# A decoder layer on one core: from unit 13 of 16 the engines' written orders put attention first, and the first half's exponents go behind the last unit

## The chip, the core and the metric

The kernel runs on one core of a Trainium2 chip. The core has five engines with a queue each: TensorE (PE, matmuls), VectorE (DVE), ScalarE (ACT), GpSimd (POOL) and SyncE (SP, which issues the transfers here). Each engine works through its own list in the order in which the program writes it, and waits for semaphores that other engines raise. The metric is the device time of one execution in microseconds (us), lower is better.

## What is computed

One decoder layer on x of 8 batches x 128 tokens x 128 features, in float32:

```python
x = x + attention(layernorm(x))          # 16 heads of 8, causal, score = -beta * distance(q, k)
x = x + mlstm(layernorm(x), ctx, ctx)    # 4 heads of 32, queries from x, keys and values from ctx
x = x + experts(layernorm(x))            # router over 8 experts, top 2, each silu(g) * u, then down
```

The score of the attention is a function of the squared distance between query and key. With `ed = sqrt(|q|^2 - 2qk + |k|^2 + eps)`, it is one of three formulas, chosen by `ed < 0.1` and `ed > 2`, and a softmax over the keys follows. The second block's weights are built from gates:

```python
log_D = cumsum(log_sigmoid(f))[t] - cumsum(log_sigmoid(f))[s] + i[s]       # for s <= t
C = (q @ k.T) / sqrt(32) * exp(log_D - max_s(log_D))
h = C / (max(|sum(C)|, exp(-max_s(log_D))) + 1e-6) @ v                     # then a norm over each head
```

The gates `i` and `f` are 8 columns of a product of [x, ctx, ctx] with a 384 x 8 matrix.

## The kernel before

**Three stages.** The attention is worked in 16 *units* (numbers 0 to 15; two units of 8 heads for each batch). Then the second block and the router are worked in two *halves* of four batches (half 0 is batches 0 to 3, half 1 is batches 4 to 7). Then 16 expert products follow: `z` 0 to 7 are the eight experts for half 0, `z` 8 to 15 those for half 1.

**The attention pipeline.** Every engine runs `step(s)` for s up to 20, and in a step each engine works on several units at different stages. The distances of unit s+1 and s+2 are made on PE (`scores`). ACT takes squares, logarithms and exponentials of them. DVE makes the chosen formula of unit s (L1011, L1018, L1036), and then the *far selection* of unit s-1 (L1071), which writes `dist`. POOL adds the causal mask to unit s-1 (L596, L599) and makes the comparison for a later one (L607). DVE takes the row minima of unit s-2 (L1030, then two small subtractions L1046, L1063). PE turns the minima (below called `minima`, into PM), ACT copies them into `shift` (L801), PE transposes `dist` and adds the shift in ten matmuls (`weights`, into P3), ACT makes the exponential (L773, `pT`), PE multiplies with the values (`values`, into PO). At the end of each batch follow on DVE a copy, a reciprocal and a product (L1004, L1021, L1040), on PE a transpose, on ACT a copy (`oT`, L778), on PE the product with `wo`, and on DVE the sum L1053 that writes a batch of the first residual, `x1`. Its statistics are `stat(b)` (L1078, L1079). All matmuls stand under L1352, the helper `mm`.

**The second block.** For half c its stages are `front(c, 0..7)`: the rstd (ACT), normed rows `xn` (L913 to L916, L951 on DVE), their transpose `xT` (PE, then L817 on ACT), the gate products from the context (`of_context`, 8 matmuls) and from the rows (8 matmuls), their sum on DVE (L1092 to L1099), three functions on ACT (L821 to L823), a difference (L1102), the cumulated sum on PE, `aT` (L1105, L1106), its transpose, a running maximum (L1112) and `rblk` (L1116, L1119). Each is one hop from engine to engine with little work in it. Then for each batch m of the half: `ex(m)` on PE (the exponents, two matmuls of 512 columns), `rows(m)` on ACT (four exponentials of 128 columns, L834), `qk(m)` on PE (128x512 in float32), `rows(m)` on DVE (the product L1130), `outs(m)` on PE (into 33 columns for each head) and `outs(m)` on ACT (L844, L845). There is one PSUM bank for `qk`, so `qk(m+1)` waits for the L1130 of batch m. When all four batches of half 0 are out, the DVE stages `head(0, 0, 0..6)` follow: denominator (L1158 to L1161), variance (L1167 to L1169), gain (L1176), root, product (L1197), the sum into `x2` (L1205), statistics (L1212, L1215). Then `back(0, 5)` makes normed rows again (L913 to L951), PE transposes them, ACT copies them and rounds them to `xhi`, DVE makes `xlo` (L1271), and the router follows.

**Where the order comes from.** The tables `ACT_AT`, `DVE_AT` and `PE_AT` say for a step and a place in it which of these stages the engine runs there; a call of `at(s, place)` does it. `(21, 1)` is the last place before the experts, `(22 + z, ...)` lies inside them. In before, half 0's `front` stages lie at steps 13 to 16, its `ex`, `qk`, `rows` and `outs` at steps 15 to 20, and `head` between the stages of `front(1, ...)` at `(20, 5)` on DVE. PE has the whole chunk 1 (`ex`, `qk`, `outs` 4 to 6) ahead of the first expert product.

**Filler matmuls.** `stay_warm(n)` on PE issues n matmuls of 512 columns that nobody reads. `WARM` gives their number ahead of `ex(4)` and of the stages 1 to 5 of `front(1, ...)`: 7, 5, 2, 6, 1, 0.

**POOL** runs its attention steps up to s = 16, copies half 0's `xT` into a block layout at s = 14 (`blocks(0)`), makes `centre(0)` at s = 16, then waits for the expert weights (`exp_in`) and splits them for z = 0, 1 (`prepare`: a cast and a subtraction of 128x512), then `blocks(1)`, `centre(1)`, and the other splits beside the experts.

## Time and profile before

| | us |
|---|---|
| median of 3 runs | 255.01 (254.7 to 256.24) |
| the profiled execution | 257.45, of which the span on the core is 255.6 |
| busy: PE, DVE, ACT, POOL | 198.8 (78%), 190.6 (75%), 157.1 (61%), 112.0 (44%) |

The chain that ended last spends 52% of the span on PE, 21% on DVE, 12% on ACT and 13% in gaps in which nothing visible was waited for. The profile page's rows of tenths give 40 slices of 6.4 us. DVE is at 9 or near it up to slice 16 (about 105 us), PE from slice 26 on (about 166 us); between these two stretches no engine is full. A time in a row is counted from the span's start; "idle before" is how long the engine stood before the row, with what ended it.

### The profile page before, as it was taken

How to read it: one execution, taken by the hardware profiler on the slowest of the kernel's cores; microseconds unless marked ns; L12 is line 12 of the kernel's file. 1: busy time of each engine (PE TensorE's matmuls, PEld its weight loads, DVE VectorE, ACT ScalarE, POOL GpSimd, SP SyncE). 2: the span in 40 equal slices, each digit the busy share in tenths (PEclk: the TensorE clock that was granted, in tenths of full speed). 3: DMA queues.
4: the chain of work that ended last, by engine and by line, in shares of the span. 5: the costliest groups of instructions: out<-in, count | busy, mean ns of one | idle time of the engine just before them, and what ended most of it. 6: DMA issues, size and time to landing. Idle time of an engine off the chain costs nothing.

```text
span 255.6 us, 6401 instructions
## 1 busy us (share of the span) xinstructions
PE 198.8 (78%) x2340; PEld 151.8 (59%) x2341; DVE 190.6 (75%) x532; ACT 157.1 (61%) x319; POOL 112.0 (44%) x151
## 2 busy tenths in 40 slices
PE   0697442744758669768798896999999898999995
PEld 0263132534546457557555752478988797888884
DVE  6868899995799999997757389673786943656554
ACT  2499989992999999785256221565555549332320
POOL 9730365673446654447126018002367744734000
PEclk9999955555897775665579868899999999999999
DMA  4305674884068149400000400000000000100001
GB/s 116 94 1 133 155 188 128 223 210 107 9 220 255 32 109 348 132 3 0 3 1 3 167 1 0 0 3 0 0 3 1 1 3 0 41 1 3 0 3 42
DMA packets 28396, 17.49 MB, mean 68 GB/s; under 512 B 11588, under 2 KB 26444, under 8 KB 28108
## 3 DMA queue, kind: packets, MB, share of 16 engines
...
## 4 chain that ended last, share of the span: by engine, by line
PE 52%; DVE 21%; issue 13%; ACT 12%; DMA 1%; DVEq 0%; ACTq 0%
PE P L1352 36%; PE PO L1352 12%; PE PM L1352 4%; DVE dist_mem L1018 3%; DVE xn L951 2%; DVE dist L1071 2%; DVE nm L1030 1%; ACT dist_mem L795 1%; DMA x_sb<-x 1%; ACT split_mem L718 1%; DVE dist_mem L1036 1%; DVE wgu L977 1%; ACT sqn L784 1%; DVE split_mem L1130 1%; DVE dist_mem L1011 1%
## 5 line engine op out<-in xcount | busy, mean ns | idle before, releaser
L1313 DVE SCALAR_TENSOR_TENSOR dist_mem<-P,gub,dist_mem 128x512 f32<-128x512 f32 x32 | 23.8, 749 | 24.8 <-ACT dist_mem L873 24.5
L873 ACT ACTIVATE dist_mem<-P,gub 128x512 f32<-128x512 f32 x32 | 21.9, 689 | 30.9 <-PE P L1352 30.9
L607 POOL TENSOR_SCALAR m_gt<-dist_mem 128x640 uint8<-128x640 f32 x16 | 29.0, 1814 | 6.0 <-issue 4.0
L1352 PEld LDWEIGHTS PO<-proj_mem,dist_mem 128*128 128x128 f32 x244 | 29.4, 192 | 1.2 <-DVE ctx_sb L1331 0.2
L1352 PE MATMUL PO<-proj_mem,dist_mem 128*128 128x128 f32 x244 | 30.0, 276 | 0.0
L1352 PE MATMUL P<-cf,dist 128*128 128x128 f32 x80 | 22.9, 369 | 6.5 <-ACT shift L801 6.5
L596 POOL TENSOR_TENSOR dist<-dist,cf 128x128 f32<-128x128 f32 x16 | 7.3, 457 | 46.6 <-DVE dist L1071 46.6
L1352 PE MATMUL P<-xhi,whi 128*128 128x512 f32 x64 | 26.5, 415 | 1.1 <-DVE dist_mem L1313 1.1
L1352 PE MATMUL P<-xhi,wlo 128*128 128x512 f32 x64 | 25.1, 392 | 0.0
L1352 PE MATMUL P<-xlo,whi 128*128 128x512 f32 x64 | 25.0, 391 | 0.0
L1352 PEld LDWEIGHTS P<-cf,dist 128*128 128x128 f32 x80 | 14.9, 186 | 12.1 <-ACT shift L801 9.5
L657 POOL TENSOR_TENSOR wlo<-wgu,whi 128x512 fp32r<-128x512 f32 x16 | 20.4, 1274 | 3.2 <-POOL whi L654 3.2
L1352 PE MATMUL P<-shift,cb 128*128 128x128 bf16 x80 | 20.6, 274 | 0.0
L654 POOL CAST whi<-wgu 128x512 fp32r<-128x512 f32 x16 | 10.3, 646 | 21.6 <-PE P L1352 21.6
L1352 PE MATMUL P<-stn,stq 128*32 128x256 bf16 (+3 forms) x256 | 10.9, 315 | 11.0 <-DVE dist_mem L1018 10.8
L1352 PE MATMUL P<-stk,stq 128*32 128x256 bf16 (+3 forms) x256 | 10.8, 311 | 10.0 <-issue 6.9
L665 POOL TENSOR_TENSOR ctx_sb<-ctx_sb,dist_mem 128x512 f32<-128x512 f32 x8 | 10.4, 1301 | 17.8 <-ACT dist_mem L881 17.8
L1352 PEld LDWEIGHTS P<-stn,stq 128*32 128x32 bf16 x256 | 7.3, 122 | 15.4 <-issue 14.8
L1030 DVE TENSOR_REDUCE nm<-dist 128x2 f32<-128x256 f32 (+1 forms) x64 | 15.5, 305 | 0.8 <-POOL dist L599 0.7
L1352 PE MATMUL PO<-vab,proj_mem 128*32 128x9 f32 (+1 forms) x896 | 13.8, 193 | 2.0 <-ACT proj_mem L773 1.9
L1352 PEld LDWEIGHTS PO<-vab,proj_mem 128*32 128x32 f32 x896 | 12.5, 132 | 3.7 <-ACT proj_mem L773 2.2
L1352 PEld LDWEIGHTS P<-stk,stq 128*32 128x32 bf16 x256 | 7.8, 129 | 11.3 <-issue 10.8
...
## 6 DMA issues: line engine op xcount, KB each, us to landing
...
```

The lines of the kernel that those rows point to most:

```text
L596: pool.tensor_tensor(ends, ends, cm.unsqueeze(1).unsqueeze(1).broadcast_to([128, 2, 2, ST]), ALU.add)
L607: pool.tensor_scalar(m_gt[:, g.k % 2, :], e2[:, g.k % 2, :], 4.0 - ATT_EPS, None, ALU.is_gt).then_inc(sm["gt_done"], 1)
L654: pool.tensor_copy(hi, w).then_inc(sm["whi_done"], 1)
L657: pool.tensor_tensor(lo, w, hi, ALU.subtract).then_inc(sm["w_ready"], 1)
L665: pool.tensor_tensor(chunk(acc, 0), chunk(acc, 0), yw[:, :, :], ALU.add).then_inc(sm["added"], 1)
L873: A(sil[:, f, :], (P1, P2)[f][:, 0, :], ACT.Silu, bias=gub[:, 0, one:one + 1]).then_inc(sm["sil_done"], 1)
L951: V.tensor_scalar(xn[:, b, :], src[:, c * CB + b, :], mv[:, p, b, 0:1], rs[:, p, 4, b:b + 1], ALU.subtract, ALU.mult).then_inc(sm["xn_done ...
L1018: V.copy_predicated(wt[:, p, :], m_ge[:, p, :], P2f).then_inc(sm["sel_done"], 1)
L1030: last = V.tensor_reduce(m[:, strip, :], strip_of(d, strip), AX.X, ALU.min, negate=True)
L1071: V.copy_predicated(dist[:, far.k % 4, :], m_gt[:, far.k % 2, :], da[:, far.k % 2, :]).then_inc(sm["dist_done"], 1)
L1313: V.scalar_tensor_tensor(hT[:, z % 2 * 2 + f, :], (P1, P2)[f][:, 1, :], gub[:, 1, one:one + 1], sil[:, f, :], ALU.add, ALU.mult).then_inc( ...
L1352: return nc.tensor.matmul(out_, lhsT, rhs, start=start, stop=stop, **more)
```

## The change

It writes the lists of all four compute engines anew from unit 13 on.

- **Half 0's gate stages** are spread over steps 13 to 19, one hop for each place: the context products in two pairs at step 14, the row products in two pairs at steps 14 and 15, the cumulated sum, transposes and maximum at steps 16 to 18.
- **Half 0's exponents** (`ex`, `qk`, `rows`, `outs` 0 to 3) move from steps 15 to 20 behind the last unit, to `(20, 2)` on PE and ACT and `(20, 5)` on DVE, between the stages of `front(1, ...)`; only `ex(0)` stays at step 18.
- **`head(0, ...)`** stood between `front(1, ...)` stages on DVE, and now stands behind `front(1, 6)`, all seven parts together.
- **The far selection of unit 15** is at the start of step 16 on DVE instead of near its end; on PE `minima(15)` is moved to the end of step 16 and `weights(15)` ahead of `values(14)`.
- **Fillers:** WARM is 6, 0, 0, 0, 0, 0, and the six write to PO after the last `x1`.
- **POOL:** `prepare(0)` runs at s = 13, `blocks(0)` and `centre(0)` at s = 16; the subtraction of the first two splits is cut in four parts of 128 columns.

```diff
-WARM = (7, 5, 2, 6, 1, 0)
+WARM = (6, 0, 0, 0, 0, 0)
...
-          (13, 7): [("front", 0, 1)], (14, 7): [("front", 0, 3)],
-          (15, 3): [("front", 0, 4), ("front", 0, 5), ("front", 0, 6)], (16, 1): [("stat", 4)],
+          (13, 7): [("front", 0, 1)], (16, 7): [("front", 0, 3)],
+          (17, 6): [("front", 0, 4), ("stat", 4), ("stat", 5)], (17, 7): [("front", 0, 5), ("front", 0, 6)],
...
+                parts = 4 if z <= POOL_BLOCKS else 1
...
+            for s in range(-1, NU + 1):
+                step(At(None, s))
+                if s in (0, 2):
+                    spread(s // 2)
+                if s == 13:
+                    pool.wait_ge(sm["exp_in"], 48)
+                    prepare(0)
+                if s == NU:
+                    blocks(0)
+                    centre(0)
...
             def step(s):
                 k_ = s.k
                 low, far, near = s - 2, s - 1, s + 1
                 t = s - 4
+                if far.k == NU - 1:
+                    far_selection(far)
...
-                if far.there():
-                    wait(dve, "ds_done", far.n(1))
-                    wait(dve, "gt_done", far.n(1))
-                    wait(dve, "da_done", far.n(1))
-                    pass_waits(dve)
-                    V.copy_predicated(dist[:, far.k % 4, :], m_gt[:, far.k % 2, :], da[:, far.k % 2, :]).then_inc(sm["dist_done"], 1)
+                if far.there() and far.k < NU - 1:
+                    far_selection(far)
...
+                if k_ == NU + 1:
+                    weights(s, s - 2)
+                values(s, s - 3)
+                at(k_, 3)
+                if k_ <= NU:
+                    minima(s, s - 2)
+                at(k_, 4)
+                if k_ <= NU:
+                    weights(s, s - 2)
+                if k_ == NU:
+                    minima(s + 1, s - 1)
...
             def stay_warm(n):
 
+                if n:
+                    pe.wait_ge(sm["x1_done"], B)
                 for _ in range(n):
-                    mm(P2[:, 0, :], ident_b, cb[:, 0:512])
+                    mm(PO[:, :], ident_b, cb[:, 0:512])
```

DVE before, in step 15 from the minima of unit 13 on; `gf`, `aT`, `runmax` and `rblk` are half 0's gates, L1036 and L1040 are attention:

```order
L1030 TENSOR_REDUCE nm<-dist 128x2 [waits nmT_full,causal_done]
L1030 TENSOR_REDUCE nm<-dist 128x2 x3
L1102 TENSOR_TENSOR gf<-gf 128x16 [waits l1p_done]
L1105 COPY gf<-P 128x16 [waits cs_full]
L1106 TENSOR_TENSOR aT<-gpre,P 128x16
L1112 SCALAR_TENSOR_TENSOR runmax<-P,cf 16x128 [waits ar_full]
L1116 TENSOR_TENSOR runmax<-runmax 16x128 [waits rm_done]
L1116 TENSOR_TENSOR runmax<-runmax 16x128 [waits chain_d]
L1119 TENSOR_TENSOR rblk<-runmax,cb 80x512 [waits chain_d]
L1036 SCALAR_TENSOR_TENSOR dist_mem<-dist_mem 128x640 [waits lp_done,sel_done]
L1040 TENSOR_TENSOR o_n<-o_sb,o_rec 128x128 [waits o_rec_done]
```

DVE after, the same place (L1040 is the minima, L1046 the product, L999 the far selection, L1063 the batch of `x1`):

```order
L1040 TENSOR_REDUCE nm<-dist 128x2 [waits nmT_full,causal_done]
L1040 TENSOR_REDUCE nm<-dist 128x2 x3
L1046 SCALAR_TENSOR_TENSOR dist_mem<-dist_mem 128x640 [waits lp_done,sel_done]
L1050 TENSOR_TENSOR o_n<-o_sb,o_rec 128x128 [waits o_rec_done]
L1056 TENSOR_TENSOR nm<-nm 128x8 [waits nm0_done]
L1063 TENSOR_TENSOR x_sb<-PM,x_sb 128x128 [waits wo_full]
L1073 TENSOR_TENSOR nm<-nm 128x8 [waits nm1_done]
L999 COPY_PREDICATED dist<-m_gt,dist_mem 128x640 [waits da_done,ds_done,gt_done] x2
```

Seven gate instructions have left the place between the minima and the product, and the far selections of units 14 and 15 stand one behind the other.

DVE before, from the last batch's statistics on (L1158 to L1169 are the head norm of half 0, L913 to L951 half 1's normed rows):

```order
L1078 BN_STATS bst<-x_sb 128x6 [waits x1_done]
L1079 BN_AGGR mv<-bst 128x2 [waits chain_d]
L1158 SCALAR_TENSOR_TENSOR hden<-split_mem,enm 128x16 [waits enm_done,hs_done]
L1159 TENSOR_TENSOR hden<-hden,split_mem 128x16 [waits chain_d]
L1160 TENSOR_SCALAR hden<-hden 128x16 [waits chain_d]
L1161 RECIPROCAL hden<-hden 128x16 [waits chain_d]
L913 TENSOR_TENSOR rs<-rs 128x4 [waits r0_done,chain_d]
L914 SCALAR_TENSOR_TENSOR rs<-mv,rs 128x4 [waits chain_d]
L915 TENSOR_SCALAR rs<-rs 128x4 [waits chain_d]
L916 TENSOR_TENSOR rs<-rs 128x4 [waits chain_d]
L951 TENSOR_SCALAR xn<-x_sb,mv,rs 128x128 [waits tr_full,chain_d]
L951 TENSOR_SCALAR xn<-x_sb,mv,rs 128x128 x3
```

DVE after, behind the same statistics (L1136 is a batch's product of half 0, L914 to L952 the normed rows of half 1, L1098 and L1099 the gate sums):

```order
L1136 SCALAR_TENSOR_TENSOR split_mem<-P,split_mem 128x512 [waits dT_done,qk2_full]
L914 TENSOR_TENSOR rs<-rs 128x4 [waits r0_done]
L915 SCALAR_TENSOR_TENSOR rs<-mv,rs 128x4 [waits chain_d]
L916 TENSOR_SCALAR rs<-rs 128x4 [waits chain_d]
L917 TENSOR_TENSOR rs<-rs 128x4 [waits chain_d]
L952 TENSOR_SCALAR xn<-x_sb,mv,rs 128x128 [waits tr_full,chain_d]
L952 TENSOR_SCALAR xn<-x_sb,mv,rs 128x128 x3
L1136 SCALAR_TENSOR_TENSOR split_mem<-P,split_mem 128x512 [waits dT_done,qk2_full]
L1098 TENSOR_TENSOR gpre<-P,gb 128x32 [waits gc_full]
L1099 COPY vmean<-P 128x16 [waits chain_d]
L1136 SCALAR_TENSOR_TENSOR split_mem<-P,split_mem 128x512 [waits hh_full,dT_done,qk2_full]
L1103 TENSOR_TENSOR gpre<-gpre,P 128x32 [waits g_full]
```

The head norm has gone from here to behind `rblk`, and the four batch products of half 0 have come in its place.

PE before, from the last product with `wo` on; `wg` is the context product of half 1, `cb` alone are fillers, `xn` the transposes of the normed rows:

```order
L1352 MATMUL PO<-wo_sb,oT 128x128 [waits oT_done]
L1352 MATMUL P<-wg,split_mem 128x12 [waits ctx_in,pT_done]
L1352 MATMUL P<-wg,split_mem 128x12 x3
L1352 MATMUL P<-cb 128x512 x5
L1352 MATMUL P<-cf,xn 128x128 [waits xn_done]
L1352 MATMUL P<-cf,xn 128x128 x3
L1352 MATMUL P<-cb 128x512 x2
L1352 MATMUL P<-wg_raw,xT 128x8 [waits pT_done,vmean_done,xT_done,ctx_in]
L1352 MATMUL P<-wg_raw,xT 128x8 x3
L1352 MATMUL P<-cb 128x512 x6
L1352 MATMUL P<-gf,tri 128x16 [waits lf_done]
L1352 MATMUL P<-cb 128x512
```

PE after, from the same product on (`split_mem` is `qk`, `cb` with `rblk` is `ex`, `ctx` is `outs`):

```order
L1358 MATMUL PO<-wo_sb,oT 128x128 [waits oT_done]
L1358 MATMUL P<-split_mem 128x512 [waits sel_done,blk_done]
L1358 MATMUL P<-cb 128x512 [waits em_done]
L1358 MATMUL P<-rblk,cb 128x512
L1358 MATMUL P<-split_mem 128x512 [waits cT_done]
L1358 MATMUL P<-ctx,split_mem 128x33 [waits cT_done,centred]
L1358 MATMUL P<-ctx,split_mem 128x33 x3
L1358 MATMUL P<-wg,split_mem 128x12 [waits pT_done,ctx_in]
L1358 MATMUL P<-wg,split_mem 128x12 x3
L1358 MATMUL P<-cf,xn 128x128 [waits xn_done]
L1358 MATMUL P<-cf,xn 128x128 x3
L1358 MATMUL P<-cb 128x512 [waits dT_done]
```

The fillers are gone, and half 0's exponents stand ahead of half 1's context product and between its later stages.

## Rows read from the trace of the kernel before

**Rows 1.** Busy time of each engine in three stretches: start:end, length, each engine.

```profile
103.50:147.30 43.80, 36.31 (x537) 26.66 (x537) 31.80 (x93) 23.50 (x62) 17.66 (x27) 0.69 0.10 37
147.30:162.40 15.10, 12.11 (x45) 5.77 (x47) 13.76 (x54) 3.29 (x13) 6.30 (x7) 0.75 0.00 1
162.40:171.40 9.00, 8.73 (x51) 5.83 (x49) 5.49 (x28) 6.16 (x22) 0.00 (x0) 1.00 0.01 2
```

**Rows 2.** Timeline of DVE, steps 13 to 15: start, us, engine, line.

```profile
109.44 1.61 DVE L951 TENSOR_SCALAR xn<-x_sb,mv,rs 128x128 f32<-128x128 f32 x4
...
117.26 0.19 DVE L1092 TENSOR_TENSOR gpre<-P,gb 128x32 f32<-128x32 f32 x1 [1.23 <-PE P L1352]
...
118.46 0.81 DVE L1011 SCALAR_TENSOR_TENSOR dist_mem<-dist_mem,P 128x640 f32<-128x640 f32 x1
...
124.24 0.81 DVE L1036 SCALAR_TENSOR_TENSOR dist_mem<-dist_mem 128x640 f32<-128x640 f32 x1
```

**Rows 3.** Timeline of DVE: far selection of unit 15, last batch of x1.

```profile
131.79 0.89 DVE L1071 COPY_PREDICATED dist<-m_gt,dist_mem 128x640 f32<-128x640 uint8 x1
...
147.03 0.29 DVE L1053 TENSOR_TENSOR x_sb<-PO,x_sb 128x128 f32<-128x128 f32 x1 [1.74 <-PE PO L1352]
```

**Rows 4.** Timeline of PE: qk twice, outs, transposes twice, the first expert product.

```profile
128.51 1.91 PE L1352 MATMUL P<-split_mem 128*128 128x512 f32 x2
...
133.81 1.12 PE L1352 MATMUL P<-split_mem 128*128 128x512 f32 x2 [0.19 <-DVE split_mem L1130]
...
144.25 1.31 PE L1352 MATMUL P<-ctx,split_mem 128*128 128x33 f32 x8
...
150.69 1.06 PE L1352 MATMUL P<-cf,xn 128*128 128x128 f32 x4
...
162.84 0.60 PE L1352 MATMUL P<-cf,xn 128*128 128x128 f32 x4
...
171.37 0.48 PE L1352 MATMUL P<-xhi,whi 128*128 128x512 f32 x1
```

**Rows 5.** Timeline of DVE, second phase: head norm, rblk, last normed rows.

```profile
147.78 0.16 DVE L1158 SCALAR_TENSOR_TENSOR hden<-split_mem,enm 128x16 f32<-128x16 f32 x1
147.98 0.18 DVE L1159 TENSOR_TENSOR hden<-hden,split_mem 128x16 f32<-128x16 f32 x1
...
155.29 0.69 DVE L1197 TENSOR_TENSOR split_mem<-split_mem 128x512 f32<-128x512 f32 x1
...
157.72 0.86 DVE L1212 BATCH_NORM_STATS2 bst<-x_sb 128x6 f32<-128x128 f32 x4
158.62 0.38 DVE L1215 BATCH_NORM_AGGREGATE mv<-bst 128x2 f32<-128x6 f32 x4
...
159.96 0.69 DVE L1119 TENSOR_TENSOR rblk<-runmax,cb 80x512 bf16<-80x512 bf16 x1
...
161.35 1.11 DVE L951 TENSOR_SCALAR xn<-x_sb,mv,rs 128x128 f32<-128x128 f32 x4
```

**Rows 6.** Timeline of ACT: rows(0), and the rstd ahead of back(0, 5).

```profile
131.86 1.09 ACT L834 ACTIVATE split_mem<-P,aT 128x128 f32<-128x128 f32 x4
...
159.10 0.30 ACT L693 ACTIVATE rs<-mv,eps_col 128x4 f32<-128x4 f32 x1 [3.40 <-DVE mv L1215]
159.43 0.21 ACT L694 ACTIVATE rs<-rs 128x4 f32<-128x4 f32 x1
```

**Rows 7.** PE in five stretches: start:end, length, busy, granted clock, DMA.

```profile
112.00:130.00 18.00, 14.92 (x180) 0.50 0.01 1
131.00:144.00 13.00, 11.56 (x228) 1.00 0.20 82
145.00:151.00 6.00, 5.35 (x20) 0.50 0.01 1
155.00:157.00 2.00, 0.03 (x1) 1.00 0.00 0
158.60:161.60 3.00, 3.00 (x8) 0.50 0.00 0
```

137 lines of the change are left out of this document (66 added, 71 removed).

## The prediction

> **What bounds the kernel now.** I read the busy times by stretch first. From step 13 to the last batch of `x1` (103.5 to 147.3 us) no engine is full: PE 36.3, DVE 31.8 and ACT 23.5 of 43.8 us; this is the *tail*, where engines hand small pieces to each other. From there to the end of the normed rows of `back(0, 5)` (147.3 to 162.4, the *second phase*) DVE is busy for 13.76 of 15.10 us. From 162.4 to the first expert product PE is busy for 8.73 of 9.00 us [rows 1]. From the first product at 171.37 [rows 4] to the end of the span, 255.6, PE is the bound (84.2 us), and its list is the same afterwards. So the change is worth what it does to the start of that product. I call the end of the last `x1` T (147.03 + 0.29, about 147.3 [rows 3]) and the end of `back(0, 5)` E (161.35 + 1.11, about 162.4 [rows 5]). The sum has three terms: the move of T, the growth of T to E, the growth of E to the product.
>
> **Term 1, the tail.** Before, DVE starts step 15 at 118.46, having waited 1.23 us for the gate products of PE and run four small gate instructions from 117.26 on. In step 15 seven gate instructions and their hops stand ahead of L1036, which starts at 124.24 [rows 2]; the far selection of unit 15 comes at 131.79, and T 15.5 us later [rows 3].
>
> After the change I walk it forward with the same durations. Step 13 ends later, since the rstd of the normed rows now stands behind ACT's place 5: about 0.7 us, so L951 ends at 109.44 + 1.61 + 0.7 = 111.8 [rows 2]. Step 14 is then 5.1 us of DVE work without a wait (before, from the end of L951 at 111.05 to the instruction ahead of the wait, 117.26 - 1.23 = 116.0: 5.0 us [rows 2]), and so is most of step 15; there DVE waits about 0.8 us for the `wo` product. Step 15 ends at about 122.7. The exponential that the far selection of unit 15 needs stands behind ACT's `shift` of unit 13 and ends at about 123.7. So this selection starts at 123.7, 8.1 us earlier. Behind it stand the minima of 14, the sum L1053 of unit 11 (it waits for PE until 127.3), half 0's gate sums (0.65) and the minima of 15, which end at 129.2. PE takes them only behind `weights(14)`, at 130.6; then come two gate hops (cumulated sum and transpose, to 132.2), `weights(15)` (1.8 at half clock), the exponential (0.8), `values(15)` with the copy ahead of it (to 136.3), a transpose, `ex(0)`, two `wo` products with their copies, each with a hop: T at 140.3. That is 16.6 us behind the selection, where before had 15.5. PE's items in this walk are at half clock, 1.2 GHz, because the granted clock was 0.50 from 112 to 130, though PE was busy for 14.9 of 18 us; it was 1.00 from 131 to 144 [rows 7], the stretch in which `qk` and `ex` of half 0 stood in the tail. The first `qk` started at 128.51 and took 1.91 us, the next 1.12 [rows 4]. These are now gone from the tail. At full clock the walk would be 2.2 us shorter. **Term 1: -7.0 us** (bounds -9.2 and -5.5, the last if the selection's 8.1 us shrink by two more waits like the 1.23 of [rows 2]).
>
> **Term 2, T to E.** Before, DVE did half 0's head norm in the gaps of half 1's gate hops, and `rblk` ended at 159.96 + 0.69 = 160.6, 13.3 us behind T [rows 5]. After, half 0's four batches go into these gaps. Walk from T: PE does `qk(0)` from T - 0.4 (1.9 at half clock), `ex(1)`, `qk(1)` behind L1130, to T + 4.1; `outs(0)` 1.3, the context product 1.0 and the transposes 0.6 follow, to T + 6.9 (kinds and half-clock times in [rows 4]). Then `ex(2)` and `qk(2)` to 8.3, `outs(1)` to 9.2, the row products to 10.3, `ex(3)` to 10.7. ACT's `rows(3)` (1.09, [rows 6]) stands ahead of half 1's three gate functions there, so these end at 12.6. Cumulated sum, `outs(2)`, transpose, `outs(3)` bring the running maximum to T + 14.4 and `rblk` to T + 16.1. Only then does the head norm run, and it is serial. It has 11 small instructions at about 0.2 each (the first two of them start 0.20 apart: 147.78, 147.98), four wide ones at 0.69, statistics 0.86 + 0.38 [rows 5], the rstd on ACT 0.30 + 0.21 [rows 6] and a hop, four small ones, and the normed rows 1.11 [rows 5]: 2.2 + 2.8 + 1.25 + 0.65 + 0.8 + 1.1 = 8.8 us. So E comes at T + 24.9, against 15.1. With PE at full clock from T the first walk is 2.3 us shorter, E at T + 22.6. I take T + 24.1, nearer to the slow end because PE enters T behind a tail of small matmuls. **Term 2: +9.0 us** (bounds +5.3, below, and +10). The fillers of this phase cost nothing where they stood: before, DVE was the full engine there.
>
> **Term 3, E to the product.** PE's list from `back(0, 5)` on is the same. What differs is what PE did ahead of it. Before, fillers kept it busy for 3.0 of 3.0 us from 158.6 to 161.6, still at 0.50, and the transposes at 162.84 then took 0.60, against 1.06 for the same work at 150.69 [rows 4, 7]. Ahead of that, an idle stretch from 155 to 157 (0.03 us busy, clock 1.00) had been followed by the 0.50 [rows 7]. After, behind the six fillers, `ex(4)` and `qk(4)`, PE has nothing for some 7 us of head norm. If the clock falls, transposes cost +0.45 on the path, one or two `qk` +0.8 each (1.91 against 1.12), `outs` +0.3. Against it, `rows(4)` and `qk(4)` are done early (-0.3). **Term 3: +1.0 us** (bounds -0.3 and +2.5).
> The Trainium skill (TensorE: Matmul & The Clock Gate, "HAM oscillation — how this bites in real kernels") says that waits between bursts of matmuls make the clock fall back to half, and that each burst then starts slow; that speaks against this change, in term 3. This trace agrees (0.50 behind the idle stretch at 155); by the rule the term is +2.0, and if the fillers still counted, -0.3.
>
> **What costs nothing.** POOL's `prepare(0)` at step 13 (0.6 + 1.3 us) lies in a stretch of the tail where POOL was idle, its masks wait for DVE and not the reverse; the weights have landed by then (the transfers' share is 0.01 from 112 us on [rows 7]). POOL is busy for 17.7 of 43.8 us in the tail [rows 1]. If the cover is gone, each mask is late by up to 2 us.
>
> **The sum.** -7.0 + 9.0 + 1.0 = +3.0 us on the profiled execution (257.45). This stands 2.4 above the median 255.0, and the difference moves both alike: 258.0.
>
> **Rivals.**
> 1. *Slower, as summed* (0.40): 256 to 260.5. For it: DVE is busy for 13.76 of 15.10 us in the second phase [rows 1], so 2.8 us of L1130 and a serial norm of 8.8 have no gap there, and each gate hop now waits behind a `qk` or an `outs` on PE. About 0.07 of it lies under 257.6.
> 2. *No change* (0.30): the mechanism of 1 with PE at full clock in the tail and from T on: -9.2 + 7.5 + 1.0 = -0.7, so 254.3 (253 to 257). For it: 1.00 from 131 to 144; against it: 0.50 from 112 to 130 and from 145 to 151 [rows 7].
> 3. *Faster: the exponents ride in the gates' gaps* (0.20). In before, the gate chain took 13.3 us from T with 7 us of norm in between. If four batches with 0.69 each on DVE make the chain no longer than 11.5 us and `outs(3)` is out by then, E is at T + 20.4, term 2 is +5.3. With -8.1 for the tail and +0.2 for term 3: -2.6, so 252.4; with the tail at -9.2, 251.3. It decides for faster when `rblk` of half 1 ends less than 12 us behind T.
> 4. *Much slower: PE stays at half clock all through the second phase* (0.10). Its items are about 12 us at full clock; 10 more would put E 6 us later: 262 to 264. Against it: `qk` and `ex` brought the clock back at 131 [rows 7].
>
> **Range and chances.** The range 252.0 to 260.5 holds 1, 2 and most of 3, and leaves out 0.07 of 3 and the 0.10 of 4. Rival 1 alone: 256 to 260.5. What a measurement can tell from no change here is about 1%, 2.55 us. Faster by more than that (under 252.5): 0.20; within it: 0.30 + 0.07 = 0.37; slower: 0.33 of 1 and the 0.10 of 4 = 0.43.
>
> **What would show each step.** Far selection of unit 15 at about 124 and T at 138 to 140.5; if T lies above 142 or below 137, term 1 is wrong. The granted clock from 113 to T at 0.50. In the second phase: `rblk` of half 1 at T + 14 to 16, DVE idle for 7 to 9 us before it, then L1158 to L951 without a gap for about 9 us. PE idle for about 7 us ahead of the transposes of `back(0, 5)`, which take 1.06 rather than 0.60. First expert product near 174.4, and 84 us from there to the end. The prediction is wrong if the norm is hidden after all, or if the product starts before 171.

## The result, and the profile after

| | before | changed |
|---|---|---|
| median of 4 executions each, us | 255.62 (254.7 to 256.54) | 268.12 (262.71 to 270.9) |
| ratio | | 1.033 (95%: 1.0213 to 1.0447) |
| the profiled execution, us | 257.45, span 255.6 | 270.84, span 268.8 |
| the same kernel once more, 4 executions | 257.38 (254.44 to 259.26, 7 executions) | 263.25 (262.37 to 270.15), ratio 1.0278 (1.0173 to 1.0384) |
| its profiled execution | | 262.37, span 260.6 |

The change makes the kernel slower, by 3% (the medians of the first row stand at 1.049). Of the eight executions of the changed kernel five took 262.4 to 265.4 us and three 270.2 to 270.9; the ratios leave these three out, and the first profile, at 270.84, is one of them. Such executions, of 267 us and more, are called *long* below. The median of the other five is 262.9, and that of the kernel before, taken in the same way over its comparisons, 256.0: the change costs 6.9 us. Two profiles are read here: the long one recorded with the result, and that of the repeat (`e10_changed_again`).

The three stretches of the prediction, with its own borders (busy us of each engine after the length, then PE's clock):

```profile
103.50:141.50 38.00, 30.44 (x499) 23.57 (x500) 28.19 (x90) 19.22 (x41) 18.48 (x33) 0.51 0.14 47
141.50:168.00 26.50, 18.85 (x79) 10.81 (x78) 16.12 (x58) 8.91 (x35) 5.29 (x7) 0.76 0.00 1
168.00:183.07 15.07, 14.92 (x48) 10.66 (x49) 6.41 (x30) 5.67 (x20) 0.00 (x0) 0.50 0.01 1
```

The tail is shorter than in [rows 1], and the two stretches behind it are longer: 26.5 us against 15.1, and 15.1 against 9.0. In the last one the clock is 0.50, where before it was 1.00.

DVE in the changed kernel (start, us, engine, line). L999 is the far selection of unit 15, L1063 the last batch of `x1`, L1108 the difference of half 1's gates, L1125 `rblk`, L1164 the first instruction of the head norm, L952 the normed rows:

```profile
125.50 0.88 DVE L999 COPY_PREDICATED dist<-m_gt,dist_mem 128x640 f32<-128x640 uint8 x1 [1.00 <-ACT dist L807]
...
141.22 0.29 DVE L1063 TENSOR_TENSOR x_sb<-PO,x_sb 128x128 f32<-128x128 f32 x1 [0.54 <-PE PO L1358]
...
153.58 1.02 DVE L1108 TENSOR_TENSOR gf<-gf 128x16 f32<-128x16 f32 x1 [2.27 <-ACT gf L824]
...
157.29 0.69 DVE L1125 TENSOR_TENSOR rblk<-runmax,cb 80x512 bf16<-80x512 bf16 x1
158.99 0.18 DVE L1164 SCALAR_TENSOR_TENSOR hden<-split_mem,enm 128x16 f32<-128x16 f32 x1 [1.02 <-ACT split_mem L846]
...
166.89 1.11 DVE L952 TENSOR_SCALAR xn<-x_sb,mv,rs 128x128 f32<-128x128 f32 x4
```

These rows answer to [rows 3, 5]. The far selection comes 6.3 us earlier (125.50 for 131.79) and T 5.8 us earlier (141.51 for 147.32). The gates of half 1 wait for ACT and PE (2.27 us ahead of L1108), `rblk` ends at T + 16.5, the head norm begins at T + 17.5 behind a wait of 1.02 for the last `outs` copy of ACT, and E is 166.89 + 1.11 = 168.0, T + 26.5.

PE in the changed kernel around the same place. 156.59 is the product of `outs(3)`, 162.03 and 169.88 are `qk(4)` and `qk(5)`, 168.15 the transposes of `back(0, 5)`, 175.69 the router's logits, 183.07 the first expert product:

```profile
154.66 0.40 PE L1358 MATMUL P<-gf,tri 128*128 128x16 f32 x2 [2.46 <-DVE gf L1108]
...
156.59 1.89 PE L1358 MATMUL P<-ctx,split_mem 128*128 128x33 f32 x8 [0.42 <-ACT split_mem L846]
...
162.03 1.42 PE L1358 MATMUL PM<-dist,split_mem 128*128 128x512 f32 x2
168.15 1.08 PE L1358 MATMUL P<-cf,xn 128*128 128x128 f32 x4 [4.70 <-DVE xn L952]
...
169.88 1.92 PE L1358 MATMUL PM<-dist,split_mem 128*128 128x512 f32 x2
...
175.69 1.71 PE L1358 MATMUL P<-rw,dist_mem 128*128 128x8 f32 x8
...
183.07 0.77 PE L1358 MATMUL P<-xhi,whi 128*128 128x512 f32 x1
```

The transposes take 1.08 us (before 0.60 [rows 4]), behind an idle stretch of 4.70. And `qk`, `outs` and the first product, for which rows at either level are there, all stand at their longer duration: 1.92, 1.75, 0.77. PE is busy for 14.92 of the 15.07 us up to 183.07, and still the first expert product comes 11.7 us later than before [rows 4].

PE's busy time and granted clock in stretches of the changed kernel:

```profile
113.00:141.00 28.00, 23.68 (x380) 18.61 (x380) 20.72 (x70) 11.68 (x28) 12.12 (x24) 0.50 0.11 39
146.00:154.00 8.00, 6.19 (x41) 4.58 (x40) 2.30 (x7) 4.21 (x16) 4.72 (x7) 1.00 0.01 2
156.00:162.00 6.00, 5.36 (x17) 2.92 (x17) 4.41 (x14) 1.42 (x6) 0.00 (x0) 0.50 0.00 0
163.00:166.00 3.00, 0.45 (x2) 0.00 (x0) 2.33 (x10) 0.45 (x3) 0.00 (x0) 1.00 0.00 0
167.00:186.00 19.00, 17.85 (x55) 13.01 (x56) 7.41 (x34) 7.49 (x24) 0.00 (x0) 0.50 0.00 1
```

The clock is at 0.50, 1.2 GHz, all through the tail (23.68 of 28 us busy), 1.00 from 146 to 154, 0.50 from 156 to 162 behind PE's wait of 2.46 for L1108, 1.00 while PE is nearly idle (163 to 166), and 0.50 again from 166 on, 2 us ahead of the transposes, to about 186.5, although PE is busy for 17.85 of the 19 us of the last row.

The repeat, PE at the same places, then two of its stretches:

```profile
155.07 1.89 PE L1358 MATMUL P<-ctx,split_mem 128*128 128x33 f32 x8 [0.41 <-ACT split_mem L846]
...
166.63 1.09 PE L1358 MATMUL P<-cf,xn 128*128 128x128 f32 x4 [5.50 <-DVE xn L952]
...
168.37 1.62 PE L1358 MATMUL PM<-dist,split_mem 128*128 128x512 f32 x2
169.82 0.98 PE L1358 MATMUL P<-ctx,split_mem 128*128 128x33 f32 x8
...
175.74 0.48 PE L1358 MATMUL P<-xhi,whi 128*128 128x512 f32 x1
```

```profile
163.00:168.00 5.00, 1.37 (x6) 1.06 (x7) 3.33 (x17) 1.78 (x7) 0.00 (x0) 0.50 0.00 0
169.00:186.00 17.00, 16.91 (x103) 13.76 (x102) 9.52 (x35) 9.84 (x30) 1.88 (x2) 0.98 0.00 1
```

Here the fall is the same (5.50 us idle, transposes 1.09), but the clock is back at about 169.6, within the next `qk` (168.37, 1.62 us), and `outs` takes 0.98. The first product comes 9.25 us behind E.

**The account, against the profile of before:**

| term | predicted | 262.37 us profile | 270.84 us profile |
|---|---|---|---|
| 1, move of T | -7.0 | -7.3 | -5.8 |
| 2, T to E | +9.0 | +11.3 | +11.3 |
| 3, E to the product | +1.0 | +0.3 | +6.1 |
| product to the end (84.2 before) | 0 | +0.6 | +1.5 |
| sum, in the span | +3.0 | +5.0 | +13.2 |

The profiles differ in T by chance too. Four kernels have the list of before up to T (before, e4, e5, e2), and their T is 147.3, 145.7, 145.8 and 146.4: the profile of before is the latest. Eight have the list of the changed kernel, and their T is 138.8 to 141.6. Mean against mean the tail is 5.9 us shorter. With that for term 1, and the other terms of the 262.37 us profile, the sum is +6.3, near the 6.9 of the medians.

### The profile page after: what moved, and what is told of

It is laid out like the page before. It is cut to its first block and busy times, and to the rows that moved or that the text cites. A ratio compares the mean times of both kernels' runs of the same rounds, so it can differ in the third digit from the quotient of the medians.

```text
span 268.8 us, 6374 instructions
## 1 busy us (share of the span) xinstructions
PE 206.0 (77%) x2325; PEld 159.2 (59%) x2326; DVE 188.7 (70%) x532; ACT 157.3 (59%) x319; POOL 111.8 (42%) x157
## 5 line engine op out<-in xcount | busy, mean ns | idle before, releaser
L1358 PE MATMUL P<-cf,dist 128*128 128x128 f32 x80 | 25.0, 394 | 6.9 <-ACT shift L802 6.9
L1358 PE MATMUL P<-xhi,whi 128*128 128x512 f32 x64 | 27.3, 427 | 1.1 <-DVE dist_mem L1319 1.1
L1358 PE MATMUL P<-xlo,whi 128*128 128x512 f32 x64 | 25.7, 401 | 0.0
L1358 PEld LDWEIGHTS P<-cf,dist 128*128 128x128 f32 x80 | 16.3, 204 | 12.3 <-ACT shift L802 9.1
L646 POOL TENSOR_TENSOR wlo<-wgu,whi 128x512 fp32r<-128x512 f32 (+1 forms) x22 | 21.2, 977 | 3.2 <-POOL whi L639 3.2
L1358 PE MATMUL P<-shift,cb 128*128 128x128 bf16 x80 | 22.4, 290 | 0.0
L1358 PE MATMUL PO<-vab,proj_mem 128*32 128x9 f32 (+1 forms) x896 | 14.8, 197 | 3.9 <-issue 2.6
L1358 PEld LDWEIGHTS PO<-vab,proj_mem 128*32 128x32 f32 x896 | 13.6, 140 | 5.6 <-issue 3.7
L774 ACT ACTIVATE proj_mem<-P,nbeta 128x640 f32<-128x640 f32 x16 | 12.6, 790 | 6.9 <-PE P L1358 6.9
L1040 DVE TENSOR_REDUCE nm<-dist 128x2 f32<-128x256 f32 (+1 forms) x64 | 15.4, 301 | 0.0
```

What stands on the lines that cost most here:

```text
L646: last = pool.tensor_tensor(lo[:, part], w[:, part], hi[:, part], ALU.subtract)
L774: A(pT[:, t.k % 2, :], P3f, ACT.Exp, scale=nbeta[:, :]).then_inc(sm["pT_done"], 1)
L1040: last = V.tensor_reduce(m[:, strip, :], strip_of(d, strip), AX.X, ALU.min, negate=True)
L1358: return nc.tensor.matmul(out_, lhsT, rhs, start=start, stop=stop, **more)
```

## The experiments

All times of a row come from its profiled execution: T (end of the last `x1`), E (end of the normed rows of `back(0, 5)`), first expert product, end of the span.

| kernel | T | E | T to E | product | E to product | span |
|---|---|---|---|---|---|---|
| before | 147.3 | 162.5 | 15.1 | 171.4 | 8.9 | 255.6 |
| changed | 141.5 | 168.0 | 26.5 | 183.1 | 15.1 | 268.8 |
| e10, changed again | 140.1 | 166.5 | 26.4 | 175.7 | 9.2 | 260.6 |
| e1, changed + 20 fillers | 139.8 | 166.3 | 26.5 | 175.0 | 8.7 | 259.1 |
| e11, changed + 6 | 138.8 | 165.4 | 26.6 | 174.2 | 8.7 | 258.2 |
| e12, changed + 12 | 140.6 | 167.1 | 26.5 | 181.3 | 14.2 | 267.2 |
| e7, e1 + 8 behind T | 141.6 | 167.3 | 25.7 | 176.0 | 8.7 | 260.1 |
| e6, e1, gates first | 140.6 | 170.5 | 29.9 | 179.2 | 8.7 | 263.3 |
| e9, e1, norm in the gates | 140.2 | 165.5 | 25.3 | 174.2 | 8.7 | 258.3 |
| e4, before, serial norm | 145.7 | 166.7 | 21.1 | 181.8 | 15.1 | 267.8 |
| e5, e4 + 24 fillers | 145.8 | 166.3 | 20.6 | 175.8 | 9.5 | 259.9 |
| e2, before, no fillers | 146.4 | 161.7 | 15.3 | 172.0 | 10.3 | 256.2 |
| e3, before, far early | 143.4 | 158.6 | 15.2 | 168.9 | 10.3 | 253.1 |
| e8, e3 + 8 fillers | 146.0 | 162.9 | 16.9 | 171.6 | 8.7 | 255.8 |

### Is the loss behind E the clock of PE?

`e1_fill_norm`: the changed kernel, with filler matmuls in the idle stretch of PE ahead of the transposes.

```diff
-(21, 1): [("front", 1, 5), ("qk", 4), ("back", 0, 5), ("ex", 5), ("qk", 5), ("outs", 4), ("ex", 6), ("qk", 6), ("back", 0, 6), ("outs", 5), ("ex", 7), ("qk", 7), ("outs", 6)],
+(21, 1): [("front", 1, 5), ("qk", 4), ("warm", 20), ("back", 0, 5), ("ex", 5), ("qk", 5), ("outs", 4), ("ex", 6), ("qk", 6), ("back", 0, 6), ("outs", 5), ("ex", 7), ("qk", 7), ("outs", 6)],
```

> The changed kernel with 20 more filler matmuls (128x512, bf16, into PO) on PE between qk(4) and the transposes of back(0, 5), where PE stood idle for 4.7 us during the serial head norm. Nothing else differs. Theory A (the idle stretch lets PE's clock fall, and the matmuls of the second half's batches and of the first expert then run at 1.2 GHz for 20 us): granted clock 1.00 from the transposes on, E to the first expert product 9 to 10 us instead of 15.1, the experts 84 instead of 85.7 us, total 6 to 8 us less than the changed kernel: about 259 to 262, and the runs lie closer together. Theory B (the fillers only add work; that stretch is bound by ACT and DVE): total unchanged or up to 1 us more, 265 to 269.

Measured: 261.1 us (260.36 to 261.49), ratio to before 1.016 (1.0084 to 1.0236). PE of this kernel, the fillers, the transposes, `qk(5)` and the first product:

```profile
161.32 4.48 PE L1358 MATMUL PO<-cb 128*128 128x512 bf16 x20
166.46 0.63 PE L1358 MATMUL P<-cf,xn 128*128 128x128 f32 x4 [0.66 <-DVE xn L952]
...
167.36 1.02 PE L1358 MATMUL PM<-dist,split_mem 128*128 128x512 f32 x2
...
175.02 0.48 PE L1358 MATMUL P<-xhi,whi 128*128 128x512 f32 x1
```

The transposes take 0.63 and `qk(5)` 1.02, and the product stands 8.7 us behind E. So theory A holds: in this profile nothing of term 3 is left, and T to E is as it was, 26.5 us. No execution is long, and the median is 1.8 us under the 262.9 of the changed kernel. It is still 1.6% slower than before, with the idle stretch all but closed (0.66 us).

`e11_fill_6` and `e12_fill_12`: the same with 6 and with 12 fillers. The edit of the first is shown; that of the second has 12 in its place.

```diff
-(21, 1): [("front", 1, 5), ("qk", 4), ("warm", 20), ("back", 0, 5), ("ex", 5), ("qk", 5), ("outs", 4), ("ex", 6), ("qk", 6), ("back", 0, 6), ("outs", 5), ("ex", 7), ("qk", 7), ("outs", 6)],
+(21, 1): [("front", 1, 5), ("qk", 4), ("warm", 6), ("back", 0, 5), ("ex", 5), ("qk", 5), ("outs", 4), ("ex", 6), ("qk", 6), ("back", 0, 6), ("outs", 5), ("ex", 7), ("qk", 7), ("outs", 6)],
```

> The changed kernel with 6 fillers (not 20) behind the fifth qk, so that PE stands idle for 3.5 to 4 us ahead of the transposes of back(0,5) instead of 4.7 to 5.5. Theory A (the clock falls in the idle hole that is left, wherever the fillers stood): transposes 1.06 to 1.09 us, E to first product 9.3 to 15 us, total 262 to 271 with a wide spread. Theory B (a short burst behind the fifth qk is enough to keep the clock up over the rest of the hole): transposes 0.63, E to product 8.7 us, total 260 to 261.5.

> The same with 12 fillers: some 2.3 us idle ahead of the transposes. Theory A, if the fall needs the longer hole: transposes 0.63, E to product 8.7 to 9.5 us, total 260 to 262, narrow spread. If even this hole is enough for the fall: 262 to 271. Theory B: 260 to 261.5.

Measured: with six 260.6 us (260.03 to 268.22), ratio 1.0192 (1.0104 to 1.0279); with twelve 264.66 us (260.34 to 269.04, 6 executions), ratio 1.0218 (1.0119 to 1.0317). The kernels e1, e5, e7 and e9, which have 20 or 24 fillers there, lie between 258.4 and 262.0 us in all of their 16 executions. But e6, with 20 as well, has one of 269.25 among its four, and its mean clock there, 0.809, is not below that of the other three (0.805 to 0.817), so that it gives no sign of a long stretch at half clock. The profile with six has 3.10 us idle ahead of the transposes, and the clock stays at 1.00:

```profile
165.59 0.63 PE L1358 MATMUL P<-cf,xn 128*128 128x128 f32 x4 [3.10 <-DVE xn L952]
```

That with twelve, PE and then two stretches:

```profile
162.21 2.75 PE L1358 MATMUL PO<-cb 128*128 128x512 bf16 x12
167.27 0.63 PE L1358 MATMUL P<-cf,xn 128*128 128x128 f32 x4 [2.31 <-DVE xn L952]
...
168.17 1.87 PE L1358 MATMUL PM<-dist,split_mem 128*128 128x512 f32 x2
...
181.32 0.77 PE L1358 MATMUL P<-xhi,whi 128*128 128x512 f32 x1
```

```profile
164.00:168.00 4.00, 1.69 (x11) 0.86 (x10) 2.97 (x15) 1.60 (x7) 0.00 (x0) 1.00 0.00 0
168.00:180.00 12.00, 12.00 (x38) 8.10 (x37) 5.03 (x28) 5.60 (x20) 0.00 (x0) 0.51 0.01 1
```

The transposes run at full clock behind 2.31 us without work, and only then, in `qk(5)` and with PE busy, the clock goes to 0.50, and stays there for 17 us, up to about 185.3. Six fillers gave theory B's numbers but for one execution of 268.22; twelve gave the times of theory A's second case, with three of six executions at 267.1 to 269.0, but not its fall in the hole. So neither theory explains both: the loss comes behind a hole of half the length too, and a longer one (e11) does not always bring it. Nor is the length of the hole what decides: e7 below has 2.41 us there and keeps its clock. What decides it stayed open.

Counted over all kernels with the serial norm: with up to 12 fillers ahead of the transposes 10 of 22 executions are long (changed, e4, e11, e12), with 20 or 24 one of 20. So the fillers take the long executions away almost wholly. The three long ones that were profiled (the changed kernel, e4, e12) all show the clock at 0.50 for 17 us or more behind E; the other eight were not profiled.

### Does the serial norm alone do it?

`e4_before_serial_norm`: the kernel before, its exponents left in the tail, but the seven parts of `head(0, ...)` behind `front(1, 6)` on DVE as in the changed kernel (and ACT's rstd ahead of them moved likewise).

```diff
-(20, 5): [("stat", 7), ("head", 0, 0, 0), ("front", 1, 1), ("head", 0, 0, 1), ("front", 1, 2), ("head", 0, 0, 2), ("head", 0, 0, 3), ("front", 1, 3), ("head", 0, 0, 4), ("front", 1, 4), ("head", 0, 0, 5), ("front", 1, 5), ("head", 0, 0, 6), ("front", 1, 6), ("back", 0, 5), ("front", 1, 7), ("rows", 4)],
+(20, 5): [("stat", 7), ("front", 1, 1), ("front", 1, 2), ("front", 1, 3), ("front", 1, 4), ("front", 1, 5), ("front", 1, 6), ("head", 0, 0, 0), ("head", 0, 0, 1), ("head", 0, 0, 2), ("head", 0, 0, 3), ("head", 0, 0, 4), ("head", 0, 0, 5), ("head", 0, 0, 6), ("back", 0, 5), ("front", 1, 7), ("rows", 4)],
```

> The kernel before with one part of the change: on DVE all seven parts of head(0, ...) stand behind front(1, 6) instead of between the front stages (and ACT's rstd for them behind front(1, 3)). Theory A (term 2 as summed: the serial norm has no cover): rblk at T + 11 to 12, then 8.8 us, E at T + 20 to 21 instead of 15.1, so +5 to +6 us, plus whatever PE's clock loses in the longer idle stretch (0 to 6): 260 to 267. Theory B (DVE's norm only moved, the gate chain becomes shorter by as much): 255 to 257.

Measured: 268.78 us (261.23 to 270.14): three of four executions are long, the fourth took 261.23, and no ratio could be given for it. The profile is one of the long ones. PE, and its clock:

```profile
166.87 1.09 PE L1352 MATMUL P<-cf,xn 128*128 128x128 f32 x4 [7.19 <-DVE xn L951]
...
168.60 1.92 PE L1352 MATMUL PM<-dist,split_mem 128*128 128x512 f32 x2
...
181.80 0.77 PE L1352 MATMUL P<-xhi,whi 128*128 128x512 f32 x1
```

```profile
156.00:162.00 6.00, 3.29 (x12) 1.04 (x10) 5.50 (x18) 0.52 (x2) 0.61 (x1) 1.00 0.00 0
163.00:166.00 3.00, 0.00 (x0) 0.00 (x0) 2.17 (x14) 1.53 (x6) 0.00 (x0) 0.50 0.00 0
167.00:182.00 15.00, 15.00 (x49) 10.71 (x50) 6.13 (x29) 5.65 (x20) 0.00 (x0) 0.50 0.00 1
```

This one edit gives the kernel before a time like the changed one's: 261.23 in the fourth execution, 5 us over before, and the same long executions. In the profile PE is idle for 7.19 us; the transposes take 1.09, `qk(5)` 1.92, and from 167 to 182 PE is busy for 15.00 of 15.00 us at 0.50. The product stands 15.1 us behind E, as in the changed kernel.

`e5_serial_norm_fill` adds 24 fillers in that stretch.

```diff
-(21, 1): [("front", 1, 5), ("qk", 4), ("back", 0, 5), ("ex", 5), ("qk", 5), ("outs", 4), ("ex", 6), ("qk", 6), ("back", 0, 6), ("outs", 5), ("ex", 7), ("qk", 7), ("outs", 6)],
+(21, 1): [("front", 1, 5), ("qk", 4), ("warm", 24), ("back", 0, 5), ("ex", 5), ("qk", 5), ("outs", 4), ("ex", 6), ("qk", 6), ("back", 0, 6), ("outs", 5), ("ex", 7), ("qk", 7), ("outs", 6)],
```

> The kernel before with the head norm behind front(1, 6) on DVE (as in e4) and 24 filler matmuls on PE between qk(4) and the transposes of back(0, 5), where e4's PE stood idle for 7.2 us. It splits e4's loss (268.8 against 256.25) in two. Theory A (most of it is PE's clock): E as in e4, 5 us later than before counted from the last x1, but E to the first expert product 9 to 10 instead of 15.1 us: 260 to 262. Theory B (the serial norm itself costs the most): 265 or more.

Measured: 261.05 us (260.73 to 261.63), ratio 1.0227 (1.0177 to 1.0277). DVE, the first instruction of the norm and the last normed rows:

```profile
157.29 0.17 DVE L1158 SCALAR_TENSOR_TENSOR hden<-split_mem,enm 128x16 f32<-128x16 f32 x1
...
165.18 1.12 DVE L951 TENSOR_SCALAR xn<-x_sb,mv,rs 128x128 f32<-128x128 f32 x4
```

It splits the loss of e4. No execution is long any more, which takes 7.7 us off the median (268.78 to 261.05), while against e4's one ordinary execution, 261.23, there is no difference. A hole of 2.01 us was left, and one `qk` behind the transposes still took 1.91. The other 5 us are the norm that no longer lies in the gaps of the gates (T to E 20.6 against 15.1; 261.05 against the 255.78 of before): theory A.

Beside e1 it also shows what the rest of the change does, all of it together. Both have the serial norm and the filled stretch; e1 has half 0's exponents behind T and the new lists of the tail, e5 has the exponents in the tail and the lists of before. T is at 139.8 and 145.8, and E is at 166.3 in both. The medians are 261.1 and 261.05. **The six microseconds that the tail gains are given back to the last one between T and E.**

### The order between T and E

`e6_gates_first`: e1, with half 1's gate products, functions and sums ahead of half 0's batches on PE, ACT and DVE, so that a gate hop does not queue behind a `qk`.

```diff
-(20, 2): [("qk", 0), ("ex", 1), ("qk", 1), ("outs", 0), ("front", 1, 1), ("ex", 2), ("qk", 2), ("outs", 1), ("front", 1, 2), ("ex", 3), ("qk", 3), ("front", 1, 3), ("outs", 2), ("front", 1, 4), ("outs", 3)],
+(20, 2): [("qk", 0), ("ex", 1), ("front", 1, 1), ("qk", 1), ("front", 1, 2), ("outs", 0), ("ex", 2), ("front", 1, 3), ("qk", 2), ("outs", 1), ("front", 1, 4), ("ex", 3), ("qk", 3), ("outs", 2), ("outs", 3)],
```

> The changed kernel with the 20 fillers of e1, and with half 1's gate stages ahead of half 0's batches in the second phase: on PE front(1, k) stands one or two places earlier against qk and outs, on ACT rows(3) behind the gate functions, on DVE front(1, k) ahead of rows. Theory A (term 2: the gate hops wait behind qk and outs on PE and behind rows on ACT, and the batches themselves are a shorter chain): rblk 2 to 4 us earlier than e1's, counted from the last x1 (15.7 there after it), and the total 1 to 3 us under e1's 261.1: 258 to 260. Theory B (the four batches through one bank of qk are themselves the chain that releases the norm): rblk earlier, but L1164 starts where it did, total 260.5 to 262.

ACT's list follows. Measured: 264.69 us (262.52 to 269.25), ratio 1.0338 (1.0271 to 1.0406). DVE:

```profile
155.43 0.69 DVE L1125 TENSOR_TENSOR rblk<-runmax,cb 80x512 bf16<-80x512 bf16 x1
...
161.46 0.18 DVE L1164 SCALAR_TENSOR_TENSOR hden<-split_mem,enm 128x16 f32<-128x16 f32 x1 [3.85 <-ACT split_mem L846]
```

`rblk` ends at T + 15.5, hardly earlier than in e1 (T + 16.4), and the norm now waits 3.85 us for the last `outs` and begins at T + 20.9. The four batches, with PE at 0.50 for most of 150 to 163 and hardly idle, are what the norm waits for; the gates are out 5.3 us before. That the one `qk` bank holds them up does not show: no `qk` from 150 on waits for DVE. Neither theory has it: E comes 3.4 us later than in e1, for which theory B had no change. How much of that is the clock (at half from 151 to 165 here, from 154 to 160 in e1) was not tested.

`e9_norm_in_gates`: e1, with the opposite. On PE the batches come first, then the cumulated sum and the transpose of the gates with six fillers ahead; on DVE the parts of the norm stand between and behind `front(1, 4)` to `front(1, 6)` (the lists of PE and ACT follow suit and are not shown):

```diff
-(20, 5): [("stat", 7), ("rows", 0), ("front", 1, 1), ("rows", 1), ("front", 1, 2), ("rows", 2), ("front", 1, 3), ("front", 1, 4), ("rows", 3), ("front", 1, 5), ("front", 1, 6), ("head", 0, 0, 0), ("head", 0, 0, 1), ("head", 0, 0, 2), ("head", 0, 0, 3), ("head", 0, 0, 4), ("head", 0, 0, 5), ("head", 0, 0, 6), ("back", 0, 5), ("front", 1, 7), ("rows", 4)],
+(20, 5): [("stat", 7), ("rows", 0), ("front", 1, 1), ("rows", 1), ("front", 1, 2), ("rows", 2), ("front", 1, 3), ("rows", 3), ("front", 1, 4), ("head", 0, 0, 0), ("front", 1, 5), ("head", 0, 0, 1), ("head", 0, 0, 2), ("front", 1, 6), ("head", 0, 0, 3), ("head", 0, 0, 4), ("head", 0, 0, 5), ("head", 0, 0, 6), ("back", 0, 5), ("front", 1, 7), ("rows", 4)],
```

> The changed kernel with a filled PE gap before back(0,5), and with the order between T and E mended: on PE the four batches of half 0 are started before the gate products of half 1, six fillers stand with the gates, the outs of a batch and the rows on ACT and DVE stand one place earlier, and the parts of the head norm are interleaved with the fronts of units 5 and 6 on DVE instead of standing behind them. Theory A (the serial norm and the late batch outs are what T to E is made of): the norm starts 3 to 4 us earlier after T than in the filled version (there T+18 to T+19) or is covered by the gates, E at T+22 to T+24 instead of T+26.5, total 257 to 259.5. Theory B (the four batches' dependence chain through one engine pair sets T to E whatever the order): E stays at T+26 and the total at 260.5 to 262.

Measured: 260.34 us (258.41 to 261.4), ratio 1.0156 (1.0056 to 1.0256). DVE:

```profile
153.39 0.18 DVE L1164 SCALAR_TENSOR_TENSOR hden<-split_mem,enm 128x16 f32<-128x16 f32 x1 [1.03 <-ACT split_mem L846]
...
158.51 0.69 DVE L1125 TENSOR_TENSOR rblk<-runmax,cb 80x512 bf16<-80x512 bf16 x1
...
164.35 1.11 DVE L952 TENSOR_SCALAR xn<-x_sb,mv,rs 128x128 f32<-128x128 f32 x4
```

The norm starts at T + 13.2 instead of T + 17.5, 4.3 us earlier. But its next part waits behind a cumulated sum that is late now, `rblk` ends at T + 19.0 instead of T + 16.4, and 6.3 us of norm stand behind it. E gains 1.2 us of the expected 2.5 to 4.5, and the time is that of e1. So this order is worth about a microsecond between T and E, where e6's cost 3.4.

`e7_fill_both`: e1 with eight more fillers behind T (`WARM` 6, 0, 0, 8, 0, 0).

> e1 with 8 more fillers on PE ahead of front(1, 3), where PE waits 2.45 us for the gate functions and the granted clock then falls to 0.50, so that outs(3) takes 1.89 instead of 0.97 us. Theory A (the clock): 1.00 until E, outs(2) and outs(3) at full clock, 0.5 to 2 us less than e1: 259 to 260.6. Theory B (the fillers stand in the way of the hop they wait beside, since 8 of them take 1.8 us of a gap of 2.45): 261 to 262.

Measured: 260.48 us (258.83 to 261.95), ratio 1.02 (1.0139 to 1.0261). The clock is 1.00 from 146 on, without the fall of 156 to 162, and T to E is 25.7 us: the stretches at half clock that e1 still has between T and E cost 0.8 us, where the prediction had 2.3 for half clock all the way. They come off at the norm, whose wait for `outs(3)` is 0.29 us here and 1.02 in e1:

```profile
158.33 0.18 DVE L1164 SCALAR_TENSOR_TENSOR hden<-split_mem,enm 128x16 f32<-128x16 f32 x1 [0.29 <-ACT split_mem L846]
```

The medians (260.48 and 261.1) do not tell the two kernels apart.

### What the tail is worth

`e3_before_far_early`: the kernel before, with only the far selection of unit 15 moved to the start of step 16.

```diff
                 t = s - 4
+                if far.k == NU - 1:
+                    wait(dve, "ds_done", far.n(1))
+                    wait(dve, "gt_done", far.n(1))
+                    wait(dve, "da_done", far.n(1))
+                    pass_waits(dve)
+                    V.copy_predicated(dist[:, far.k % 4, :], m_gt[:, far.k % 2, :], da[:, far.k % 2, :]).then_inc(sm["dist_done"], 1)
...
                 at(k_, 6)
-                if far.there():
+                if far.there() and far.k < NU - 1:
```

> The kernel before with one part of the change: DVE's far selection of unit 15 stands first in step 16 instead of at place 6. Theory A (the tail's gain comes mostly from this selection no longer waiting behind the minima and the sum of unit 11): it starts about 4 us earlier (near 127.5 instead of 131.8) and the last x1 comes 2 to 4 us earlier: 251.5 to 253.5. Theory B (the gain comes from the gate stages having left steps 14 and 15; PE's weights of unit 14 hold the rest up anyway): less than 1 us, 254 to 255.

Measured: 256.27 us (254.96 to 259.09, 10 executions), ratio 1.0006 (0.9961 to 1.005). In the profile T and E come 3.9 us earlier, but PE loses 1.4 us behind E:

```profile
159.86 1.06 PE L1358 MATMUL P<-cf,xn 128*128 128x128 f32 x4
...
168.86 0.48 PE L1358 MATMUL P<-xhi,whi 128*128 128x512 f32 x1
```

The transposes take 1.06, as they run at 0.50. `e8_before_far_warm` adds eight fillers to those of the second phase (`WARM` 7, 5, 2, 14, 1, 0).

> The kernel before with the early far selection of e3 and 14 instead of 6 fillers ahead of front(1, 3), to cover PE's idle 2.1 us there. Theory A (e3's earlier tail was given back because the transposes of back(0, 5) and the first batches behind them ran at half clock): clock 1.00 around E, 1.5 to 3 us less than before: 253 to 255 against 256.25. Theory B (the fillers delay the gate hop or the early selection is worth nothing): within 1 us of before.

Measured: 255.91 us (253.11 to 257.63, 6 executions), ratio 0.9996 (0.9941 to 1.0051). E to the product is 8.7 us, and the transposes take 0.63; but in this profile the far selection is at 126.89 and T at 146.0, so the early T of e3 (124.68, 143.4) was not seen again, though the two kernels are the same up to there. The granted clock from 110 to 130 was 0.66 in e3 and 0.53 in e8. In neither kernel is a gain measured. The selection is 7.1 and 4.9 us earlier than in the profile of before, but T comes 18.7 and 19.1 us behind it, where it was 15.5; what holds it up there was not looked into. And the eight fillers of e8 are not free: behind E they give back e3's 1.6 us, but T to E is 16.9 for 15.2.

`e2_before_nofill`: the kernel before with `WARM` all zero.

> The kernel before with WARM all zero, so without its 21 filler matmuls. Theory A (clock): PE is nearly idle through the second phase, its clock is 0.50 behind E, and E to the first expert product grows from 9.0 to 12 to 15 us: 258 to 263. Theory B (fillers cost nothing and give nothing): 254.5 to 255.5.

Measured: 258.18 us (256.72 to 261.07, 10 executions), ratio 1.0067 (1.0028 to 1.0106). The clock is 0.50 from 145 to 162, T to E is the same (15.3 us), and E to the product is 10.3 for 8.9. So the loss behind E is theory A's, at less than half its size. The fillers of before are worth about 1.7 us, 1.4 of it behind E.

`e10_changed_again`: nothing edited; its numbers stand in the section on the result.

> The changed kernel once more, nothing edited, for its spread and a second profile. Theory A (the clock of PE stays at half for a stretch behind E, of a length that differs by the run): total between 262 and 271, spread of its runs several times that of the kernel before, E to first expert product 10 to 16 us, and in the profile a stretch at 0.50 that begins in the idle hole before back(0,5). Theory B (the long stretch at 0.50 was an accident of one profiled execution): the profile shows 1.00 again within 5 us of E and a total of 260 to 262.

Of its two theories neither has it alone: the profile shows the clock back 3.1 us behind E, and yet one of its four executions took 270.15.

## Why the prediction was right or wrong

The likeliest case, slower with the norm uncovered, is what happened, but the time of 258.0 and the upper end of 260.5 are both too low: even the shortest of the eight executions took 262.37.

**Term 1 held.** T came 7.3 us earlier in one profile and 5.8 in the other, against 7.0. The walk put the far selection at 123.7 and T at 140.3; the repeat has 124.06 and 140.06. In the other profile all is 1.4 us later from ahead of the far selection on (125.50, 141.51). The walk behind the selection had 16.6 us and both profiles have 16.0. The clock was 0.50 from 113 us to T, as assumed. But that -7.3 lies so near to -7.0 is in part luck: mean against mean of the profiles with either list, the move is -5.9, inside the bounds, and the term was about 1 us too large.

**Term 2 is the step that failed, by its size.** Its mechanism stands: the norm is one serial piece behind `rblk`, 9.0 us from L1164 to the end of L952 in the changed kernel, where the walk had 8.8. The walk gave E at T + 24.9, and I took 24.1 and called +10 the upper bound. Measured is T + 26.5 (+11.3). The 1.6 us over the walk (26.5 against 24.9) are 0.4 in the gates (`rblk` ends at T + 16.5 for 16.1), 1.0 of wait for `outs(3)`, and 0.2 in the norm. The missing wait is the mistake: two chains meet at the norm, the gates and the four batches. The walk had `outs(3)` in PE's list, but not the norm's own wait for ACT's copy of it. Its product ran at 0.50 (1.89 us), and the copy came behind `rblk`; with the clock at 1.00 in e7 the wait is 0.29 us. The 0.8 us I took off for a clock that might be full was a guess against my own walk, and the bound had no room for a wait at all. With 26.5 in place of 24.1 the sum is +5.4, which is 262.9 on the profiled execution, 0.5 from the repeat's 262.37. This nearness too is in part luck, since it sets the profile of before with the latest T against the shortest execution of the changed kernel. Put on the 255.0 of the forecast it is 260.4, against the 262.9 of the executions that are not long. Of these 2.5 us about 1 is the median of before (256.0 over its comparisons, not 255.0), and about 1 is term 1.

**Term 3 had the right cause, and missed the long executions.** The transposes took 1.08 and 1.09, as said. In the repeat the rest was less than taken, +0.3 in all, because only one `qk` was slow and the early `qk(4)` gave some back. In the other profile, of a long execution, it was +6.1, and +1.5 more in the expert products: the clock did not come back for 20 us. That the change makes some executions 7 to 8 us longer than others no rival had. The prediction took for granted that once PE is busy it gets its clock back soon, from [rows 7] (0.50 at 112 to 130, 1.00 from 131) and from the transposes of 162.84 [rows 4]. Rival 4 had half clock for the wrong stretch, between T and E, where PE waits anyway (0.8 us in e7 against e1); behind E, where PE is the bound, it costs 7 to 8 in a long execution (the profile of e4 against that of e5).
The Trainium skill (TensorE: Matmul & The Clock Gate, "Part 1: The HAM clock gate (the "warmup" mystery)") says that a PE that is kept busy is given the full clock. This case's traces differ: PE was busy for 15.00 of 15.00 us in e4 and stayed at 0.50. The same section says that the point of the switch differs by run, by about half a microsecond; here it comes 3.1 us behind E in one profile of the changed kernel and 18.5 in the other, far more than that.

**The rivals.** *No change* fell with the measured T to E: even with PE at full clock behind T (e7) it is 25.7 us. *Faster* needed `rblk` less than 12 us behind T; it was 16.5 and 16.4. PE stood idle for 4.70 and 5.50 us ahead of the transposes, not 7, because `qk(4)` ended later than I had it.

**What was to cost nothing.** `prepare(0)` ran at 112.08 us without a wait for the weights and took 0.64 + 1.71 us, and the next mask waited 4.32 us for DVE, not for it. The reading beside it was wrong: the transfers' share is 0.01 from 112 to 130, but 0.20 from 131 to 144 [rows 7].

**What the change adds up to.** The serial norm costs about 5 us (e5 against before). All the rest of the change comes to nothing beside it: six microseconds less tail, six more behind it (e1 against e5); its parts were not run one by one. The idle PE costs 1.8 us (e1's 261.1 against 262.9), and in a long execution 7 to 8 more. No kernel here beats before.
